# Attention and quantised FFN on one core: the row order of the stacked q and k operands, and the pattern of the loads that fill them

## The reference, cut to what matters

```
q = layernorm(x); k = v = ctx                      # per batch: (64 channels, 256 positions)
qk  = einsum('bhdq,bhdl->bhql', qh, kh) / sqrt(8)  # 8 channels d per head
ret = einsum('bhql,bhdl->bhdq', softmax(qk), vh)
x   = x + gamma * ret
h   = silu(bit_linear(xn, w_gate)) * bit_linear(xn, w_up)
x   = x + bit_linear(rms_norm(h, ln_weight), w_down)
```

## Time and profile before

| | |
|---|---|
| median of 3 runs | 218.69 us (218.49 to 219.09) |
| the profiled execution | 218.52 us |
| its span in the profile | 216.7 us |
| PE busy | 166.3 us, 77% of the span |
| VectorE, ScalarE, GpSimd busy | 151.9, 141.2, 105.1 us |
| read from and written to the chip's memory | 15.20 and 4.19 MB |

### The profile page before, as it was taken

One profiled execution on the slowest core, in us unless ns is written; L12 is line 12 of the kernel. 1 busy time (PEld: TensorE's weight loads), 2 busy tenths in 40 slices (PEclk: granted clock), 3 DMA queues, 4 the chain that ended last, 5 costly groups with the idle time before them and its releaser, 6 DMA issues.

```text
span 216.7 us, 4308 instructions
## 1 busy us (share of the span) xinstructions
PE 166.3 (77%) x1378; PEld 97.9 (45%) x1378; DVE 151.9 (70%) x287; ACT 141.2 (65%) x286; POOL 105.1 (49%) x275
## 2 busy tenths in 40 slices
PE   0008629674969896899899899989989987974963
PEld 0003214332757553475466467556556644523412
DVE  2549906443597976768997998898899796156382
ACT  3220136983657887577888778779688877973531
POOL 4403242419863829772653565284264456345250
PEclk9999999975899999589999999999999999999799
DMA  4945589671112721162025006104300000000000
GB/s 146 321 141 157 149 257 367 255 214 31 28 46 64 207 54 48 49 200 76 0 73 152 27 22 182 51 0 137 113 0 5 0 28 8 20 5 0 27 0 24
DMA packets 15714, 19.95 MB, mean 92 GB/s; under 512 B 2604, under 2 KB 14012, under 8 KB 14684
## 3 DMA queue, kind: packets, MB, share of 16 engines
q1 hardware_dynamic: 11753, 14.94, 23.4%
q10 hardware_dynamic: 3939, 4.74, 6.6%
HBM read 15.20 MB, written 4.19 MB: 90 GB/s over the span
## 4 chain that ended last, share of the span: by engine, by line
PE 38%; POOL 20%; issue 12%; DVE 11%; DMA 9%; ACT 5%; ACTq 1%; SPq 1%; POOLq 0%; DVEq 0%
PE psO L462 9%; PE psA L428 8%; PE psB L446 6%; POOL hw L332 6%; DMA q_stack<-mt 5%; DVE mneg L761 3%; PE psG L564 3%; PE psG L534 2%; PE psG L554 2%; POOL hrms L989 2%; DVE h L851 2%; DMA q_stack<-q_scratch 2%; DMA q_scratch<-q_parts 2%; DVE gu L840 2%; ACT th L682 2%
## 5 line engine op out<-in xcount | busy, mean ns | idle before, releaser
L761 DVE TENSOR_REDUCE mneg<-psA 128x2 f32<-128x512 f32 x128 | 81.8, 678 | 22.1 <-PE psA L428 22.1
L608 ACT ACTIVATE probs<-psB 128x512 f32<-128x512 f32 x128 | 73.2, 597 | 12.3 <-PE psB L446 11.8
L428 PE MATMUL psA<-k_stack,q_stack 72*128 72x256 bf16 x256 | 54.3, 303 | 16.9 <-DMA q_stack<-q_scratch 16.9
L446 PE MATMUL psB<-q_stack,k_stack 75*128 75x256 bf16 x256 | 51.4, 285 | 9.1 <-DMA q_stack<-mt 7.1
L462 PE MATMUL psO<-probs,vt 128*32 128x256 f32 x512 | 37.7, 416 | 1.0 <-ACT probs L608 1.0
L428 PEld LDWEIGHTS psA<-k_stack,q_stack 72*128 72x128 bf16 x256 | 22.9, 104 | 34.0 <-issue 25.5
L332 POOL TENSOR_TENSOR hw<-h,lnw 128x512 f32<-128x512 f32 x15 | 19.1, 1274 | 34.9 <-DVE h L851 26.5
L446 PEld LDWEIGHTS psB<-q_stack,k_stack 75*128 75x128 bf16 x256 | 24.2, 102 | 21.6 <-DMA q_stack<-mt 7.9
L462 PEld LDWEIGHTS psO<-probs,vt 128*32 128x32 f32 x512 | 14.1, 115 | 15.2 <-issue 7.9
L840 DVE SCALAR_TENSOR_TENSOR gu<-th,psG 128x512 f32<-128x512 f32 x15 | 10.3, 687 | 9.3 <-ACT th L682 9.3
L682 ACT ACTIVATE th<-psG,tscale 128x512 f32<-128x512 f32 x15 | 10.3, 688 | 8.0 <-PE psG L534 8.0
(11 more groups left out here) (133 smaller groups left out, 261.6 us busy)
## 6 DMA issues: line engine op xcount, KB each, us to landing
k_stack<-k_scratch SPq DMA_DIRECT2D x21, 192.0 KB
q_stack<-q_scratch SPq DMA_DIRECT2D x21, 192.0 KB
q_scratch<-q_parts SPq DMA_DIRECT2D x24, 64.0 KB, 3.1
k_scratch<-k_parts SPq DMA_DIRECT2D x18, 64.0 KB, 3.0
w_sb<-in_L_ffn_w_gate_dram ACTq DMA_DIRECT2D x1, 1024.0 KB, 7.8
w_sb<-in_L_ffn_w_up_dram ACTq DMA_DIRECT2D x1, 1024.0 KB, 10.8
w_sb<-in_L_ffn_w_down_dram ACTq DMA_DIRECT2D x1, 1024.0 KB, 9.0
out_dram<-y_sb SPq DMA_DIRECT2D x8, 128.0 KB, 1.8
```

The source lines that it names most:

```text
L428: mm = pe.matmul(psA[n % A_BANKS][:, qt * L:(qt + 1) * L], q_stack[0:STACK, t % NBUF, bh, qt * P:(qt + 1) * P], k_stack[0:STACK, t % NBUF, ...
L446: mm = pe.matmul(psB[b % 2][:, lt * L:(lt + 1) * L], k_stack[:, t % NBUF, bh, lt * P:(lt + 1) * P], q_stack[:, t % NBUF, bh, :], start=Tru ...
L608: act.activation(probs[:, b % RING, :], psB[b % 2][:, :], ACT.Exp, scale=SCALE).then_inc(s_exp, 1)
L761: dve.tensor_reduce(mneg[:, k % MBUF, QT * (bh % HALF):QT * (bh % HALF + 1)], psA[n % A_BANKS][:, :].rearrange("p (q l) -> p q l", q=QT), ...
```

## The change

The rows of the stacks get another order: row p now stands for (part of k p // 24, channel (p mod 24) // 3, part of q p mod 3). The scratch of k has the part outermost, so that its 24 rows (part, channel) follow each other. A k load, now one for each part a of q, reads these 24 rows once each, 192 KB in all, and writes the rows a, a+3, a+6 and so on of `k_stack`. A q load, now one for each part c of k, reads the same 24 rows as before and writes the 24 neighbouring rows 24c to 24c+23 of `q_stack`. The number of loads, their bytes and their places in the queues are the same. As every k load now needs all three parts, ScalarE's queue waits for all three stored k parts of tile 0 ahead of its first k load.

```diff
-    k_scratch = nc.dram_tensor("k_scratch", (T, DH, PARTS, BH, L), BF16, kind="Internal").ap()
+    k_scratch = nc.dram_tensor("k_scratch", (T, PARTS, DH, BH, L), BF16, kind="Internal").ap()
...
-            src, dst = ((k_parts, k_scratch), (q_parts, q_scratch))[k]
+            src, dst = ((k_parts, k_scratch[t, c]), (q_parts, q_scratch[t, :, c]))[k]
...
-            eng.dma_start(dst[t, :, c].rearrange("d b l -> b d l"), src[:, t, c, :]).then_inc(done, DMA)
+            eng.dma_start(dst.rearrange("d b l -> b d l"), src[:, t, c, :]).then_inc(done, DMA)
...
-        def load_k(eng, t, c, units, done):
-            row = k_scratch[t, :, c, units].rearrange("d b l -> d (b l)")
-            eng.dma_start(k_stack[c:STACK:PARTS, t % NBUF, units].rearrange("p b l -> p (b l)"),
-                          row.unsqueeze(1).to_broadcast([DH, PARTS, row.shape[1]])).then_inc(done, DMA)
+        def load_k(eng, t, a, units, done):
+            rows = k_scratch[t, :, :, units].rearrange("c d b l -> (c d) (b l)")
+            eng.dma_start(k_stack[a:STACK:PARTS, t % NBUF, units].rearrange("p b l -> p (b l)"),
+                          rows).then_inc(done, DMA)
...
         def load_q(eng, t, c, units, done):
-            rows = q_scratch[t, :, :, units].rearrange("d c b l -> (d c) (b l)")
-            eng.dma_start(q_stack[c:STACK:PARTS, t % NBUF, units].rearrange("p b l -> p (b l)"),
+            rows = q_scratch[t, :, :, units].rearrange("d a b l -> (d a) (b l)")
+            eng.dma_start(q_stack[REP * c:REP * (c + 1), t % NBUF, units].rearrange("p b l -> p (b l)"),
                           rows).then_inc(done, DMA)
...
             for c in range(PARTS):
                 act.wait_ge(s_kst0[c], DMA)
+            for c in range(PARTS):
                 load_k(act, 0, c, slice(0, HALF), s_first)
```

## The result

| | before | after |
|---|---|---|
| median of 6 runs each | 218.61 us | 221.01 us (218.9 to 223.89) |
| ratio after to before | | 1.0074, 95% interval 1.0038 to 1.011 |
| the profiled execution, its span | 218.52, 216.7 us | 219.89, 218.1 us |

A forecast was written before the change was run, and what follows sets the result against it. The prediction took loads to matter only at PE's start and the first maxima's landing. Terms of +0.2 (wait), -0.3 (balance) and +0.1 (neighbours) gave 0.0 us, so 218.7 us, range 217.2 to 220.0.

The forecast's parts named there:

- What bounds the kernel: Whole kernel: loads count only where PE waits for them; a shift of the first B scores at 31.23 reaches the end.
- PE's two places: Tile 0: PE's start at 16.93, after the last q load, and the landing of the first maxima loads at 31.19.
- the second wait for maxima: PE's wait ending at 41.93; left out because ScalarE was busy until 43.5, leaving 1.3 us to spare.
- Part 1, the wait: Start of tile 0: first k load moves from 9.84 to 10.65; cost +0.2 us, bounds zero and 0.4.
- Part 2, the k loads: Start and first maxima landing: better balance over 12 engines gains -0.3 us; bounds nothing, or -0.49 and -0.99.
- Part 3, the neighbours: Start and tile 1's stream: q loads into 24 neighbours cost +0.1 us; bounds zero, or +0.3 and +0.6.
- Part 4: Scratch of k: a store fills 64 KB in one piece; taken as nothing, at most some 0.1 us either way.
- The sum: Whole kernel: wait, balance and neighbours add to 0.0 us, so 218.7 us; chance 0.43.
- rival B: Start slips and tile 1's stream slows: +1.3 us, 220.0 us, first PE matmul at 17.6 or later; chance 0.20.
- Rival A: Start and first maxima landing: k loads' balance pays in full, -1.3 us, 217.4 us; chance 0.30, a good part included.

The follow-up runs named there:

- k part with its wait: Kernel before, with k loads reading 24 rows once and the wait for all three stored k parts; q loads as before, scores other numbers: ratio 1.0000.
- q part alone: Kernel before, with only the q loads changed to write 24 neighbouring rows; k loads as before, no added wait, scores other numbers: ratio 1.0167.
- with the stream lightened: Kernel before with changed k loads and their wait, q loads as before, and the norm weights' load moved from half step 30 to 50: ratio 0.9882.
- the run with the split k loads: Kernel before, from tile 1 on rows reordered, all loads into every third row, two of three k loads split; norm weights' load at half step 50: 0.9968.
- the wait alone: Kernel before, with only the three waits for stored k parts put ahead of all three first k loads: ratio 1.0008.
- the two later comparisons: The changed kernel itself, unaltered, timed twice more against the kernel before: ratios 1.0019 and 1.0009.
- the fastest correct kernel: Kernel before, from tile 1 on k parts 0 and 1 stored twice, all loads into every third row; norm weights' load at half step 50: 0.9923.

## Why the prediction was wrong, by its own steps

The step that failed is the pricing of parts 2 and 3. I took the faster k loads at -0.3 us and the q loads into neighbours at +0.1; at the first B scores the runs showed -1.8 us for the k part with its wait, and +2.6 for the q part alone. Both mechanisms were on my list, the sizes were off by far, and so was the range built from them. The first comparison, 1.6 us slower, is not explained by these parts: they nearly cancel, and it did not come back.

**What bounds the kernel.** Right that only the loads around PE's two places at the start count, and that the stack loads of later tiles are hidden in the changed kernel: its list of waits has none. That a shift of the first B scores reaches the end in full was wrong for a gain, and with it that I left out the second wait for maxima. Its 1.3 us to spare is cover against a loss. For a gain it is a cap: the load came 1.75 us earlier and the wait ended 0.6 us earlier. The k part alone gave 1.8 us at the first B scores and 0.0% in total; with the stream lightened, 1.2%. That the weights' stream sets this wait fits most of the runs and is not shown, as the run with the split k loads has it otherwise. For a loss it held: the q part's 2.6 us reached the scaling of the weights in full (50.33 against 47.73).

**Part 1, the wait.** Priced at +0.2 with 0.4 as its upper end, measured +0.8 at the first maximum by itself and +0.5 with the quicker k loads. The +0.4 to +1.4 of the changed kernel are not the wait alone, since the q part by itself makes +1.0 there. I named VectorE's third parts as queued behind the wait, and stopped there. The 2.6 us of statistics and the first maximum stand behind them in the same queue. They had no slack at all before.

**Part 2, the k loads.** Priced at -0.3 over both places, with -0.49 and -0.99 as the bounds at the start and at the landing. Measured against the wait alone: -1.5 us at the first A scores (16.07 against 17.55) and -1.9 us at the landing (3.3 against 5.2), both beyond the bounds, in single traces whose scatter is up to 0.9 us. The other kernels with such k loads and no neighbours landed in 3.9 to 5.5 us. I had taken the q loads' 15.9 GB/s per engine for a limit of the total. The two rows were no clean comparison: the window from 130.3 to 131.8 already holds q loads, and from 131 to 132 the kernel before moved 246 GB/s at a share of 0.75, 20 GB/s for each busy engine. With the k part the k stretch rose from 160 to 205 GB/s.

**Part 3, the neighbours.** Priced at +0.1, with +0.3 and +0.6 as the bounds at the start and at the landing. Measured in the q part alone: +1.0 us at the first A scores, about +1.9 us at the landing (7.2 against 5.3), and 145 against 202 GB/s in the steady part. I had hoped that three loads into different thirds of the rows even out; at 145 GB/s with all three under way they did not. The rule of the Trainium skill that I weighed ("SBUF — State Buffer", "Door 1: The DMA port swizzle") gave an estimate of 163 GB/s, and the trace of the q part alone, 145, sides with it against my +0.1. My further remark that this page would explain why 12 engines did no better than 8 does not follow: with 10 ports at some 27 GB/s each its rule gives an estimated 270 GB/s for either load, above both 175 and 191. The engine rule of the Trainium skill ("DMA: Bandwidth & Descriptors", "Why a DMA increments its semaphore by 16 and not by 1") agrees as well: the k stretch's share rises from 0.45 to 0.75.

**Part 4** was not tested by itself. The third k store took 4.9, 4.8 and 4.6 us to land in the three traces of the changed kernel, and 4.8 before, which leaves it at nothing.

**The sum.** The forecast of no change rested on small terms. In truth terms of -1.8 and +2.6 us meet at the first B scores, and where the two later comparisons agree with the forecast, that is luck. The first comparison lies beyond the range and near rival B, at 220.0. B's mechanism, a late start and slow neighbours, is present: its sign, a first matmul at 17.6 or later, stands in two of three traces (17.79, 18.34; 17.37 in the first). Rival A's mechanism stands against it. Why the first comparison stood 0.5% above the two later ones is not settled. The runs of the unchanged kernel that its ratio counts lay between 218.1 and 219.1 us, those of the later ones between 217.6 and 221.5, so I read it as scatter, which is argued, not shown. The exact share of the wait in the total stays open too: 1.0008 with an interval of 0.4% to both sides.

## What to carry to other kernels

Follow a delayed instruction through every queue that it feeds, to the end, and not only along the path that the profile's chain names; a second path can be level with it to 0.02 us. Slack behind a wait protects against losses but caps gains: before pricing a gain, look for the next wait and what sets it. Trace the unchanged kernel twice before reading differences of half a microsecond, and split a change into its parts even when the total looks flat: here they were -1.8 and +2.6 us at the first B scores, and the k part, with its stores and the norm weights arranged around it, led to the fastest correct kernel (0.9923).

## What the runs showed of the hardware

Three loads, each into 24 neighbouring partitions, ran at 145 GB/s where three into every third of 72 ran at 202, with the same 0.75 share of the DMA engines (q part alone, and before). In the changed kernel, behind the new k loads, they ran at 169 and 164. They were issued in less time: three in 1.27 us on SyncE's queue, against 2.23. Two loads into every second partition and one into neighbours cost nothing that could be told (0.998, by 4 of 12 runs). Loads from 24 separate source rows in place of 8 rows read three times raised the engines' share from 0.45 to 0.65 and the rate from 160 to 205 GB/s (k part alone). Small loads of 4 KB in another queue took 3.3 to 7.2 us to land; the shortest was beside quick k loads, the longest beside q loads into neighbours, and two traces of one kernel differed by 0.9.
